# Attention to experts: norm, transposes and splits by token tile, first experts' weights split during attention, router and choice beside the first experts

## What is computed

```python
x = x + attention(layernorm(x), ctx)
xt = layernorm(x)
logits = xt @ router_w + router_b
scores = softmax(logits) + router_bias
g = scores.reshape(T, 4, 4)                  # keep the 2 groups with the highest maximum
idx = top_k(masked, 2)                       # and in them the 2 best experts of 16
gate = zeros(T, 16).at[rows, idx].add(scores[idx])
for e in range(16):
    h = silu(xt @ w1[e] + b1[e]) * (xt @ w2[e] + b2[e])
    y = y + gate[:, e:e+1] * (h @ w3[e] + b3[e])
z = silu(xt @ sw1 + sb1) * (xt @ sw2 + sb2) @ sw3 + sb3
x = x + y + z
```

## Time and profile before

| | us |
|---|---|
| median of 3 runs (lowest, highest) | 910.67 (909.2, 914.12) |
| the execution profiled: its time | 910.75 |
| its span | 908.9 |
| TensorE busy | 744.9 (82%) |
| VectorE busy | 704.3 (77%) |
| ScalarE busy | 528.6 (58%) |
| GpSimd busy | 499.8 (55%) |

### The profile page before, as it was taken

The page is one execution under the profiler, slowest core; times in us unless marked ns, Lnnn a source line. Parts: engine busy times, 40 slices in busy tenths (PEclk is TensorE's granted clock), DMA queues, the critical chain, the costliest instruction groups (busy, mean ns, idle before and its releaser), DMA issues.

```text
span 908.9 us, 15108 instructions
## 1 busy us (share of the span) xinstructions
PE 744.9 (82%) x3482; PEld 352.1 (39%) x3483; DVE 704.3 (77%) x1432; ACT 528.6 (58%) x955; POOL 499.8 (55%) x472
## 2 busy tenths in 40 slices
PE   0379789677675076789999999999999768999997
PEld 0135444333232032334444444444444333444443
DVE  6976768788998973578888888888888656666666
ACT  3333457688774260467777777777776533455551
POOL 3953645653763700278878888888875321434341
PEclk9779979899888578989999999999999878999999
DMA  7210023121101003056666666666656620323321
GB/s 303 70 58 0 1 58 116 50 66 46 36 0 55 38 0 112 15 94 149 149 147 147 149 145 160 156 139 142 147 103 143 136 69 1 105 104 104 104 69 46
DMA packets 147599, 84.82 MB, mean 93 GB/s; under 512 B 137185, under 2 KB 137441, under 8 KB 144626
## 3 DMA queue, kind: packets, MB, share of 16 engines
q1 hardware_dynamic: 147570, 84.47, 36.0%
HBM read 49.85 MB, written 1.05 MB: 56 GB/s over the span
## 4 chain that ended last, share of the span: by engine, by line
PE 64%; DVE 19%; issue 6%; POOL 4%; ACT 3%; DMA 2%; DVEq 2%; POOLq 0%; ACTq 0%; SPq 0%
PE ps L908 20%; PE ps L909 20%; PE ps L910 19%; DVE arena L1228 5%; DVE arena L1225 4%; ACT arena L583 2%; DVE mm L1332 2%; PE ps L1102 1%; DVE arena L1222 1%; DVE mm L1331 1%; DVE dsc L1255 1%; PE ps L975 1%; POOL arena L477 1%; DVE dsc L1225 1%; POOL arena L542 1%
## 5 line engine op out<-in xcount | busy, mean ns | idle before, releaser
L908 PE MATMUL ps<-arena 128*128 128x512 f16 (+1 forms) x988 | 386.0, 391 | 32.5 <-POOL arena L401 11.4
L909 PE MATMUL ps<-arena 128*128 128x512 f16 (+1 forms) x988 | 386.1, 391 | 0.0
L910 PE MATMUL ps<-arena 128*128 128x512 f16 (+1 forms) x988 | 384.4, 389 | 0.0
L583 ACT ACTIVATE arena<-arena 128x512 f32 (+5 forms) x383 | 255.2, 690 | 135.4 <-DVE arena L1228 36.7
L1228 DVE SCALAR_TENSOR_TENSOR arena<-ps,arena 128x512 f32<-128x512 f32 (+2 forms) x186 | 125.7, 702 | 41.2 <-ACT arena L583 29.1
L908 PEld LDWEIGHTS ps<-arena 128*128 128x128 f16 (+1 forms) x988 | 99.0, 100 | 151.0 <-issue 29.4
L910 PEld LDWEIGHTS ps<-arena 128*128 128x128 f16 (+1 forms) x988 | 99.1, 100 | 124.0 <-issue 13.1
L909 PEld LDWEIGHTS ps<-arena 128*128 128x128 f16 (+1 forms) x988 | 98.8, 100 | 112.6 <-issue 10.3
L542 POOL TENSOR_SCALAR arena<-arena,rden 128x512 f32<-128x512 f32 x128 | 115.2, 900 | 30.6 <-DVE rden L1593 21.4
L1222 DVE TENSOR_TENSOR arena<-arena 128x512 f16<-128x512 f32 (+3 forms) x154 | 117.5, 795 | 7.2 <-ACT arena L583 6.4
L822 ACT ACTIVATE arena<-arena,mneg 128x512 f32<-128x512 f32 x128 | 91.4, 715 | 34.5 <-DVE mneg L1573 34.5
(11 more groups left out here) (114 smaller groups left out, 765.2 us busy)
## 6 DMA issues: line engine op xcount, KB each, us to landing
arena<-in_moe_w SPq DMA_DIRECT2D x18, 768.0 KB, 4.4
arena<-in_ffn_w SPq DMA_DIRECT2D x33, 256.0 KB, 2.7
arena<-in_wq SPq DMA_DIRECT2D x8, 1024.0 KB, 5.1
arena<-in_wo SPq DMA_DIRECT2D x8, 1024.0 KB, 5.2
arena<-in_kv_w SPq DMA_DIRECT2D x4, 1024.0 KB, 4.9
arena<-in_ctx SPq DMA_DIRECT2D x1, 2048.0 KB, 9.2
arena<-in_ctx_t SPq DMA_DIRECT2D x1, 2048.0 KB, 13.6
arena<-arena SPq DMA_TRANSPOSE x128, 3.3
```

Source lines behind the costliest of these rows:

```text
L583: return a.activation(out_, in_, ACT.Copy, scale=scale, bias=bias)
L908: pe.matmul(out_, lhs[0], rhs[0], start=first, stop=False)
L909: pe.matmul(out_, lhs[0], rhs[1], start=False, stop=False)
L910: return pe.matmul(out_, lhs[1], rhs[0], start=False, stop=last)
```

## The change

Every instruction of the router and of the experts is kept; they are put in another order, and some are divided by tile.

- ScalarE: `scale(0)`, `high_in(0)`, `high_out(0)` stand between the attention steps of units 30 and 31, with a wait for the last q product; `scale(1)` and `high_in(1)` behind step 31, ahead of `o_high(31)`. Instead of a column at a time, the transposed tiles are copied a token tile at a time. Exp of the router comes after Sigmoid of expert 0, and the copy of the gates after expert 3's step.
- GpSimd: `low_in(0)` stands between the two attention steps; `low_out(0)` behind step 31; the power is split into tiles 0 to 2 and tile 3, with `low_in(1)` between.
- VectorE: the router's weights are split ahead of step 31. Statistics and norm of tiles 0 to 2 come before `o_low(31)`, those of tile 3 after the last `add_out`. Logits after expert 0's step, scores and group choice after the adds of expert 0, expert choice after the adds of expert 1, ahead of expert 3's step; b3 after the adds of expert 2.
- TensorE: transposes of tiles 0 to 2 ahead of project(31), of tile 3 behind it; the router after hidden(0), into bank 7; the gates' transposes after experts_out(2), b3's products after hidden(4), ahead of experts_out(3).
- SyncE is unchanged, but its loads of weights for expert 3 and on wait for GpSimd's `low_out`, which is earlier for expert 0.

```diff
 (GpSimd)
+            attention_step(HK - 1, 1, False)
+            attention_step(HK - 1, 2, False)
             low_in(0, 0)
+            attention_step(HK - 1, 3, False)
             low_out(0, 0)
-            rstd(3)
+            rstd(3, 0, NT - 1)
             low_in(1, 1)
+            rstd(4, NT - 1, NT)
 (ScalarE)
+            attention_step(HK - 1, 1, False)
+            attention_step(HK - 1, 2, False)
             scale(0)
+            a.wait_ge(a_q, HK * NT)
             high_in(0, 0)
             high_out(0, 0)
+            attention_step(HK - 1, 3, False)
             scale(1)
             high_in(1, 1)
-            hidden_high(2, SX)
-            a.wait_ge(r_sub, 1)
-            a.activation(lg, lg, ACT.Exp).then_inc(r_exp, 1)
+            o_high(HK * NT - 1)
+            for t in range(NT):
+                a.wait_ge(xe_ps, t + 1)
+                copy(xt[0][:, :, t * P:(t + 1) * P], quarters(bank(t)), SX).then_inc(xe_hi, 1)
+            def router_exp():
+                a.wait_ge(r_sub, 1)
+                a.activation(lg, lg, ACT.Exp).then_inc(r_exp, 1)
...
             expert_step(0, 0)
+            router_exp()
             expert_step(0, 1)
-            with a.Fori(1, EX // 2 - 1) as j:
+            expert_step(1, 0)
+            expert_step(1, 1)
+            gates_out()
+            with a.Fori(2, EX // 2 - 1) as j:
 (TensorE)
             project(HK - 1, 2)
             values(HK - 1, 3)
+            for t in range(NT - 1):
+                expert_transposes(t)
             project(HK - 1, 3)
-            hidden_transposes(2)
-            pe.wait_ge(xt_lo, 3 * KD)
-            pe.wait_ge(r_ws, 2)
+            expert_transposes(NT - 1)
...
+            def expert_transposes(t):
+                pe.wait_ge(xe_ready, t + 1)
+                for k in range(KD):
+                    mm = pe.transpose(bank(t)[:, k * P:(k + 1) * P], xn[:, t, k * P:(k + 1) * P], ident[:, :])
+                mm.then_inc(xe_ps, 1)
...
+            pe.wait_ge(xe_lo, NT)
             hidden(0, 0)
+            router()
             hidden(1, 1)
+            experts_out(0, 0)
+            for e in range(1, 3):
+                hidden(e + 1, (e + 1) % 2)
+                experts_out(e, e % 2)
             pe.wait_ge(gates_ready, 1)
+            pe.wait_ge(m_x, 2 * NT + 2)
             for t in range(NT):
                 mm = pe.transpose(bank(5)[0:NE + 1, t * P:(t + 1) * P], gts[:, t, 1:EX], ident[:, :])
             mm.then_inc(g_t, 1)
+            hidden(4, 0)
             pe.wait_ge(g_c, 1)
             for t in range(NT):
+                pe.wait_ge(m_x, 2 * NT + t + 1)
                 pe.matmul(bank(4 + t), gt[0:NE + 1, 0, t * P:(t + 1) * P], b3[0:NE + 1, 0], start=True,
                           stop=True).then_inc(b3_ps, 1)
-            experts_out(0, 0)
-            with pe.Fori(0, EX // 2 - 1) as j:
+            experts_out(3, 1)
+            hidden(5, 1)
+            experts_out(4, 0)
+            with pe.Fori(2, EX // 2 - 1) as j:
 (VectorE)
+            attention_step(HK - 1, 3)
+            add_out(HK - 1, 2)
+            def statistics(lo, hi):
+                v.wait_ge(a_x, HK * NT - NT + hi)
+                for t in range(lo, hi):
+                    own.mark(v.bn_stats(st6[:, t], xres[:, t]))
...
+            def expert_norm(k, lo, hi):
+                v.wait_ge(rstd_ready, k + 1)
+                for t in range(lo, hi):
+                    ts(xn[:, t], xres[:, t], mv[:, t, 0:1], ALU.subtract, rs[:, t:t + 1], ALU.mult).then_inc(xe_ready, 1)
+            def expert_low(t):
+                v.wait_ge(xe_hi, t + 1)
+                piece = [w[:, :, t * P:(t + 1) * P] for w in xt]
+                stt(piece[1], quarters(bank(t)), SX, piece[0], ALU.mult, ALU.subtract).then_inc(xe_lo, 1)
+            statistics(0, NT - 1)
+            for h in range(R):
+                v.wait_ge(a_tr[h], 16 * HK * NT)
+            expert_norm(3, 0, NT - 1)
+            o_low(HK * NT - 1)
             for t in range(NT - 1):
+                expert_low(t)
             add_out(HK - 1, 3)
+            statistics(NT - 1, NT)
+            expert_norm(4, NT - 1, NT)
+            expert_low(NT - 1)
...
             expert_step(0, 0)
+            router_logits()
+            expert_step(0, 1)
+            expert_add(0, 0)
+            router_scores()
+            group_choice()
+            expert_step(1, 0)
+            expert_add(0, 1)
+            expert_choice()
+            expert_step(1, 1)
+            v.wait_ge(gates_ready, 1)
+            expert_add(1, 0)
             for t in range(NT):
                 v.wait_ge(b3_ps, t + 1)
                 stt(xres[:, t], bank(4 + t), 1.0, xres[:, t], ALU.mult, ALU.add).then_inc(b3_x, 1)
             v.wait_ge(b3_x, NT)
-            with v.Fori(0, EX // 2 - 1) as j:
+            expert_step(2, 0)
+            expert_add(1, 1)
+            with v.Fori(2, EX // 2 - 1) as j:
```

More of the change, by code:

```diff
@@ L551, in _ @@
                     attention_step(j, s)
-            for s in range(1, 4):
-                attention_step(HK - 1, s, False)
             def low_in(e, q):
@@ L838, in _ @@
                     attention_step(j, s)
-            for s in range(1, 4):
-                attention_step(HK - 1, s, False)
-            o_high(HK * NT - 1)
             def scale(e):
@@ L1160, in _, with router @@
                 attention_step(HK - 1, s)
+            def expert_transposes(t):
[3 more added lines that the diff above has]
+                mm.then_inc(xe_ps, 1)
             project(HK - 1, 2)
             values(HK - 1, 3)
+            for t in range(NT - 1):
+                expert_transposes(t)
             project(HK - 1, 3)
-            hidden_transposes(2)
-            pe.wait_ge(xt_lo, 3 * KD)
-            pe.wait_ge(r_ws, 2)
-            for t in range(NT):
+            expert_transposes(NT - 1)
+            def router():
+              pe.wait_ge(r_ws, 2)
+              for t in range(NT):
                 for k in range(KD):
@@ L1193, in experts_out @@
                         pe.wait_ge(m_x, (e - 1) * NT + t + 1)
-                    else:
+                    elif t == NT - 1:
+                        pe.wait_ge(r_sub, 1)
+                    if isinstance(e, int) and e == 3:
                         pe.wait_ge(b3_x, t + 1)
@@ L1246, in _, with norm_var @@
             v.wait_ge(q_consts, 1)
-            def norm_var():
-                ts(ve[:, :], mv[:, :, 1], EPS, ALU.add).then_inc(var_ready, 1)
+            def norm_var(lo=0, hi=NT):
+                ts(ve[:, lo:hi], mv[:, lo:hi, 1], EPS, ALU.add).then_inc(var_ready, 1)
             def block_maxima(n):
@@ L1612, in _ @@
             own.loop(1, HK - 1, 4, four_steps)
-            for s in range(1, 4):
+            for s in range(1, 3):
                 attention_step(HK - 1, s)
-            add_out(HK - 1, 2)
-            o_low(HK * NT - 1)
             v.wait_ge(in_mp, 16 * 5)
@@ L1623, in _ @@
             tt(flat(rw[1]), flat(rw_raw), flat(rw[0]), ALU.subtract).then_inc(r_ws, 1)
-            v.wait_ge(a_x, HK * NT - 1)
+            attention_step(HK - 1, 3)
[4 more added lines that the diff above has]
+                    own.mark(v.bn_stats(st6[:, t], xres[:, t]))
+                own.wait(own.n)
+                for t in range(lo, hi):
+                    own.mark(v.bn_aggr(mv[:, t], st6[:, t]))
+                own.wait(own.n)
+                norm_var(lo, hi)
+            def expert_norm(k, lo, hi):
+                v.wait_ge(rstd_ready, k + 1)
+                for t in range(lo, hi):
+                    ts(xn[:, t], xres[:, t], mv[:, t, 0:1], ALU.subtract, rs[:, t:t + 1], ALU.mult).then_inc(xe_ready, 1)
[8 more added lines that the diff above has]
+            o_low(HK * NT - 1)
             for t in range(NT - 1):
-                own.mark(v.bn_stats(st6[:, t], xres[:, t]))
+                expert_low(t)
             add_out(HK - 1, 3)
[L1630 to L1637, removed]
+            statistics(NT - 1, NT)
+            expert_norm(4, NT - 1, NT)
+            expert_low(NT - 1)
+            own.mark(v.memset(gts[:, :, 0:NS], 1.0))
+            own.mark(v.memset(gsc[:, :, 0:NS], 1.0 / SXW))
             def over(w, n):
@@ L1642, in _, with router_logits, router_scores @@
             rb, rbias = (rbb[:, i].unsqueeze(1).broadcast_to([P, NT, NE]) for i in range(2))
[L1643 to L1651, removed]
+            def router_logits():
+                v.wait_ge(r_ps, 1)
+                own.link(stt(lg, bank(7)[:, 0:NT * NE].rearrange("p (a b) -> p a b", a=NT), 1.0 / SXW, rb, ALU.mult,
+                             ALU.add))
+                own.link(v.tensor_reduce(lmax, lg, AX.X, ALU.max))
+                tt(lg, lg, over(lmax, NE), ALU.subtract).then_inc(r_sub, 1)
+            def router_scores():
+                v.wait_ge(r_exp, 1)
+                own.link(v.tensor_reduce(lsum, lg, AX.X, ALU.add))
+                own.link(v.reciprocal(linv, lsum))
+                own.link(tt(score, lg, over(linv, NE), ALU.mult))
```

(13 more changed lines are left out.)

15 lines of the change are left out of this document (5 added, 10 removed).

## The result

The changed kernel takes 920.94 us (median, 920.54 to 925.15) against 911.28 us: a ratio of 1.012 with a 95% interval of [1.0093, 1.0147]. It is slower, by 9.7 us; the forecast was 919.7 us, 9.05 more. Its profiled execution has a span of 919.2 us, 10.3 more than that of the kernel before.

A forecast was written before the change was run, and what follows sets the result against it. The bound was taken to be the serial chain between attention and experts, up to experts_out(3)'s end; +1.0 to hidden(0) and +8.05 from there gave 910.67 + 9.05 = 919.7 us, range 911.5 to 924 (likeliest 916 to 922).

The forecast's parts named there:

- Copies ahead of Exp: End of attention: three ScalarE copies put Exp of unit 31 at 721.2, not 719.6, and add_out(30) at 733.3, not 731.99.
- Norm ahead of o_low: Before the last projection: three VectorE norms take 3.24 us, o_low(31) ends at 741.6, project(31) starts at 742.75, not 736.2.
- project(31) wholly at the lower level, 5.1 us: Last projection: after TensorE's idleness all of project(31) runs at the 1.2 GHz clock, 5.1 us, ending at 747.85.
- From there to hidden(0), 6.1: End of project(31) to hidden(0): add_out, tile 3's statistics, norm, transposes, copy and split take 6.1 us, against 14.0 before.
- The wait for the gates: TensorE before the gates' transposes: stands 8.5 us for VectorE's queue, until 40.8 us after hidden(0) starts.
- the two table loads: ScalarE around the router's Exp: two loads of 1.28 us each, with no draining counted.
- The blocking of VectorE by GpSimd in the choice: VectorE's choice among the experts: operations with two SBUF inputs wait 0.45 and 0.85 us beside GpSimd's subtractions.
- b3: TensorE ahead of experts_out(3): four b3 products take 3.6 us at the upper clock level, against 5.75 before at 0.63.

The follow-up runs named there:

- hidden(4) first: Changed kernel with hidden(4) ahead of TensorE's wait for the gates: 918.79 us, ratio 1.0078; with b3 in f16 as well: 912.19 us, ratio 1.0014.
- the attention half with such orders mended: Changed kernel with weights' copies behind step 31, o_low(31), project(31) and low_in(1) earlier, router, choice, b3 as before the change: 903.39 us, ratio 0.9903.
- the attention half alone: Changed kernel with router, choice, gates and b3 ahead of the experts again, as before the change: 912.5 us, ratio 1.000.

## Why the prediction was right

All times here are from the start of values(29).

- **Copies ahead of Exp.** Exp of unit 31 at 8.53 (forecast 8.7), GpSimd's normalisations at 10.41 (10.35), add_out(30) at 21.35 (20.8). The 0.55 that is missing is the low split beside low_out(0), which I had not put next to each other: the kernel with the copies later has them apart, and the split takes 0.7 less.
- **Norm ahead of o_low.** Three norms 3.15 (3.24), project(31) at 30.1 (30.25). That the first of them waits for low_in(1) is shown by the kernel with low_in(1) early. The Trainium skill (SBUF — State Buffer, SBUF: two separate sides) has an exclusive lock on the port pair that VectorE and GpSimd share; 1.46 against 3.15 agrees.
- **project(31) wholly at the lower level, 5.1 us.** This term was mis-sized: four matmuls ran low, it took 3.5 and ended at 33.6, 1.75 earlier than I had it.
- **From there to hidden(0), 6.1.** (The terms listed in the forecast come to 6.0.) It was 5.3: the power of one tile took 0.55 us, where I had taken the 1.02 of four, and the four transposes 0.66, not 0.92. So hidden(0) began at 38.89 and not at 41.45, 2.55 too late in the forecast.
- **The wait for the gates.** hidden(0) to the gates' transposes 40.3 (40.8), the wait 8.49 (8.5), the two table loads 1.28 each with no gap. That VectorE's queue sets it is shown by the kernel with the choice left out, and that TensorE's order allows it by hidden(4) first. The blocking of VectorE by GpSimd in the choice was forecast at 0.45 and 0.85. No experiment isolates it, but the rows bear it out: two operations of the scores (at 772.21) took 1.03 us instead of 0.48, and the four large ones of the choice, each time with a GpSimd subtraction beside them, 5.71 instead of 4.9 (the 5.39 of the earlier trace rows less its two small ones). GpSimd loses too: its low_out at 781.12 took 3.36 us, and 1.20 in the kernel with the choice left out.
- **b3.** This term was mis-sized too: 4.20 instead of 3.6, and 2.75 more for the thirteen matmuls at the lower level behind it, which the forecast did not have at all. The earlier trace rows had it to be read: 772.8 to 775.4 at 0.51, after b3 products and with no pause between. I counted it as what was left of the pause.

The two errors nearly cancel: the passage was forecast 2.55 too long, and Q, at 155.9 + 8.05 = 163.95 (155.9 was the time from hidden(0) to the end before) against 166.40 measured, 2.45 too short. That is luck. Without the first error the forecast would have been 917.15, 3.8 below the measured time, and without the second 922.15, 1.2 above it, both still within the range of 911.5 to 924. The mechanism of each half was right, but for the clock behind the b3 products.

## What to carry to other kernels

Moving work off one engine's critical stretch pays only if the queue that it is put into has room ahead of the next instruction someone waits for: the choice of 10.9 us went from beside hidden(0) and hidden(1), which needed nothing of VectorE, into a queue with steps and adds of three experts, and TensorE waited 8.5 us as before. An instruction that another engine waits for (o_low(31), hidden(4)) goes ahead of independent work of the same engine, and the attention half with such orders mended is 1% faster than the kernel before (ratio 0.9903), where as written it was worth nothing. Judge such edits by landmarks within the profile, for the stretch ahead of them varied by 9 us between executions (712.50 before, 710.2 to 719.3 in the others).

## What was not expected of the hardware

Four f32 products of 17 rows by 512 columns (eight matmul instructions) are followed by a granted clock of 0.50 to 0.60, although TensorE works on without a pause. All eleven kernels with them show it, those in which the clock was at or near 1.00 during the products too (0.50 behind them in the kernel with low_in(1) early, 0.55 in the attention half alone). Of the three with f16 products two show 1.00 there, and the third (hidden(4) first) shows the lower level for seven matmuls, from 1.8 us after the end of a pause of 3.3 us on. A fall of that kind, some time after a pause, needs no f32 products: project(30) of the changed kernel began at the upper level after 4.33 us without work and fell 1 us later. What speaks for the products is the two pairs of kernels that differ in nothing but their type (and the copy that makes it), 8.49 us of pause ahead of the gates in both kernels of the one and 0.8 and 1.0 us ahead of b3 in the other: with f32 the clock fell behind them, with f16 it did not. Between six and fourteen matmuls are at the lower level, which costs 1.3 to 3.0 us; the 2.75 of the changed kernel are nearly as much as the products' own 4.2 against 1.0. Why the f32 products do that stays open, and so does whether it is the type or the longer time with 17 rows, 3.7 to 7.2 us against 1.0 to 1.4.
